# Causal attention in post-layernorm block: the diagonal key tiles of a group are taken between the full ones

## What is computed

```
q = (x @ wq_w.T + wq_b).reshape(b, t, H, HD)      # H = 32, HD = 32
k1, v1 = one key head and one value head
scores = einsum('bqhd,bkd->bhqk', q, k1) / sqrt(HD)
scores = where(causal, scores, -inf)
weights = softmax(scores)
attn = einsum('bhqk,bkd->bqhd', weights, v1).reshape(b, t, H * HD)
x = layernorm(x + attn @ wo_w.T + wo_b)
out = x_sim @ w_sim * (1 / (x_scale * w_scale))   # x and weight scaled to 448 and clipped
x = layernorm(x + out)
```

## Time and profile before

| | us |
|---|---|
| median of 3 runs | 2735.11 |
| lowest, highest | 2733.13, 2735.16 |
| the profiled execution | 2732.4 |
| its span, first to last instruction | 2730.7 |

### The profile page before, as it was taken

One profiled execution on the slowest core, in us unless ns is written; L12 is line 12 of the kernel. 1 busy time (PEld: TensorE's weight loads), 2 busy tenths in 40 slices (PEclk: granted clock), 3 DMA queues, 4 the chain that ended last, 5 costly groups with the idle time before them and its releaser, 6 DMA issues.

```text
span 2730.7 us, 45644 instructions
## 1 busy us (share of the span) xinstructions
PE 2538.9 (93%) x15400; PEld 1587.0 (58%) x15400; DVE 1876.7 (69%) x1432; ACT 1274.1 (47%) x1571; POOL 865.2 (32%) x572
## 2 busy tenths in 40 slices
PE   7999996889999999999888999999999997699998
PEld 5888884545544444444554555444444446588887
DVE  6343335657888889999555778888899993444444
ACT  2222213555566667777335555666677670100000
POOL 2321302424322222122333334222212213466663
PEclk9999997999999999999988999999999998799999
DMA  7343325512111110110333112111101004122221
GB/s 237 118 146 139 115 108 170 137 40 70 39 48 50 47 39 20 31 39 28 86 89 100 51 58 55 44 39 39 39 28 39 29 11 154 49 90 85 92 92 62
DMA packets 78776, 201.47 MB, mean 74 GB/s; under 512 B 8672, under 2 KB 10720, under 8 KB 76512
## 3 DMA queue, kind: packets, MB, share of 16 engines
q1 hardware_dynamic: 51360, 140.01, 17.8%
q10 hardware_dynamic: 27328, 60.30, 5.8%
HBM read 125.83 MB, written 74.45 MB: 73 GB/s over the span
## 4 chain that ended last, share of the span: by engine, by line
PE 77%; issue 7%; DVE 5%; ACT 4%; POOL 3%; DMA 3%; ACTq 1%; SPq 1%; DVEq 0%; POOLq 0%
PE bank L1172 16%; PE bank L1184 15%; PE bank L1083 14%; PE bank L1160 14%; PE bank L1269 13%; ACT prob L703 4%; PE bank L1202 2%; DVE acc L948 2%; DMA q_st<-max_d 2%; PE bank L1194 2%; POOL prob L540 1%; PE bank L1258 1%; DVE acc L945 1%; PE bank L1069 1%; DMA xt_raw<-x_t 1%
## 5 line engine op out<-in xcount | busy, mean ns | idle before, releaser
L703 ACT ACTIVATE prob<-bank 128x1024 f32<-128x1024 f32 (+3 forms) x1280 | 1077.6, 897 | 622.4 <-PE bank L1172 589.7
L948 DVE TENSOR_TENSOR acc<-acc,prob 128x2048 f32<-128x2048 f32 (+3 forms) x512 | 1093.1, 2135 | 130.2 <-POOL prob L540 84.9
L1172 PE MATMUL bank<-q_st,k_st 98*128 98x512 f32 (+3 forms) x2560 | 709.9, 391 | 104.3 <-ACT prob L703 62.5
L1172 PEld LDWEIGHTS bank<-q_st,k_st 98*128 98x128 f32 x2560 | 425.8, 191 | 407.0 <-ACT prob L703 310.0
L1184 PE MATMUL bank<-prob,v_sb 128*32 128x512 f32 (+3 forms) x5120 | 595.9, 547 | 11.0 <-POOL prob L540 10.8
L540 POOL TENSOR_SCALAR_AFFINE_SELECT prob<-prob 128x512 f32<-128x512 f32 x256 | 300.4, 1177 | 882.8 <-ACT prob L703 882.2
L1083 PE MATMUL bank<-xt_hi,w_hi 128*128 128x512 f32 x576 | 228.4, 397 | 16.3 <-DVE xt_lo L790 15.6
L1083 PE MATMUL bank<-xt_hi,w_lo 128*128 128x512 f32 x576 | 227.4, 395 | 0.0
L1083 PE MATMUL bank<-xt_lo,w_hi 128*128 128x512 f32 x576 | 227.3, 395 | 0.0
L1184 PEld LDWEIGHTS bank<-prob,v_sb 128*32 128x32 f32 x5120 | 107.7, 109 | 197.0 <-issue 139.2
L1269 PE MATMUL bank<-wf_hi,xs_hi 128*128 128x512 f32 x512 | 202.5, 396 | 0.0
(11 more groups left out here) (118 smaller groups left out, 2664.9 us busy)
## 6 DMA issues: line engine op xcount, KB each, us to landing
q_st<-q_hi_d SPq DMA_DIRECT2D x128, 256.0 KB
xt_raw<-x_t SPq DMA_DIRECT2D x16, 1024.0 KB, 7.0
q_hi_d<-part_hi ACTq DMA_DIRECT2D x64, 256.0 KB, 2.1
q_lo_d<-part_lo ACTq DMA_DIRECT2D x64, 256.0 KB, 2.3
q_st<-q_lo_d SPq DMA_DIRECT2D x64, 256.0 KB
x<-x_d SPq DMA_DIRECT2D x32, 512.0 KB, 3.2
out<-y ACTq DMA_DIRECT2D x32, 512.0 KB, 2.6
res<-x SPq DMA_DIRECT2D x24, 512.0 KB, 3.4
```

What stands on the lines that cost most here:

```text
L703: nc.scalar.activation(prob[:, t % SLOTS, 2 * p:2 * p + 2, off:NB], bank[:, 2 * p:2 * p + 2, off:NB], ACT.Exp, scale=SCALE).then_inc(p_don ...
L948: nc.vector.tensor_tensor(acc[:, r, :, off:NB], acc[:, r, :, off:NB], new, ALU.add).then_inc(acc_done, 1)
L1172: last = nc.tensor.matmul(bank[:, h, off:NB], k_st[:, t * P:(t + 1) * P], q_st[:, slot, h, off:NB], start=True, stop=True)
```

## The change

`key_order(j)` is a table of the order in which the key tiles of a group are taken. For j = 0 it is as before. For j > 0 the four diagonal tiles get the places 1 + (2i + 1)(n - 2) // 8 of n = 4(j + 1), the full ones fill the rest in their order. A place t now means: scores and weighing read the keys and values of tile `key_order(j)[t]`; the slot, the semaphores and the steps go by the place. `first_query` and the waits for `masked` ask whether the tile at this place is a diagonal one. On POOL the subtraction that gives `att_lo` moves from the head of the pair to behind the second mask of r = 0.

```diff
--- before.py
+++ after.py
@@ -285,9 +285,20 @@
 
             return b * (TT - QT) + (j - 1) * QT + gp
 
+        def key_order(j):
+
+            n = key_tiles(j)
+            places = {1 + (2 * i + 1) * (n - 2) // 8: QT * j + i for i in range(QT)} if j > 0 else {}
+            before = iter(range(n if j == 0 else QT * j))
+            return [places[t] if t in places else next(before) for t in range(n)]
+
+        def diagonal(j, t):
+
+            return key_order(j)[t] - QT * j
+
         def first_query(j, t):
 
-            return P * max(0, t - QT * j)
+            return P * max(0, diagonal(j, t))
 
         def pairs_of_groups(eng, b, body):
 
@@ -527,18 +538,19 @@
                 def body(j, gp, first, last):
                     if j > 0:
                         tile = projected(b, j, gp)
-                        wait_apart(pool, att_hi_cut, tile + 1)
-                        heads = att[:, (j - 1) % 2 * G:(j - 1) % 2 * G + G, bass.ds(gp * P, P)]
-                        nc.gpsimd.tensor_tensor(att_lo[:], heads, att_hi[:].bitcast(F32), ALU.subtract).then_inc(att_cut, 1)
                     for r in range(2):
                         n, s0 = group(b, j, gp, r), step(b, j, gp, r)
                         for i in range(QT):
-                            t = QT * j + i
+                            t = key_order(j).index(QT * j + i)
                             off = first_query(j, t)
                             wait_apart(pool, p_done, s0 * 2 + (2 * t + 4))
                             tri = prob[:, t % SLOTS, :, off:off + P]
                             nc.gpsimd.affine_select(out=tri, in_=tri, compare_op=ALU.is_ge, fill=0.0, base=0,
                                                     pattern=[[0, HG], [1, P]], channel_multiplier=-1).then_inc(masked, 1)
+                            if j > 0 and r == 0 and i == 1:
+                                wait_apart(pool, att_hi_cut, tile + 1)
+                                heads = att[:, (j - 1) % 2 * G:(j - 1) % 2 * G + G, bass.ds(gp * P, P)]
+                                nc.gpsimd.tensor_tensor(att_lo[:], heads, att_hi[:].bitcast(F32), ALU.subtract).then_inc(att_cut, 1)
                         if j > 0 and r == 0:
                             pool.wait_ge(res_in, stored_alone(b, j, gp) * 16 + 16)
                             nc.gpsimd.tensor_tensor(res[:], res[:], bo[:], ALU.add).then_inc(res_ready, 1)
@@ -935,8 +947,8 @@
                             off = first_query(j, t)
                             if t >= 1:
                                 dve.wait_ge(p_done, s0 * 2 + (2 * t + 4))
-                                if t >= QT * j:
-                                    dve.wait_ge(masked, n * QT + (t - QT * j + 1))
+                                if diagonal(j, t) >= 0:
+                                    dve.wait_ge(masked, n * QT + (diagonal(j, t) + 1))
                                 new = prob[:, t % SLOTS, :, off:NB]
                                 if t == 1:
                                     if off > 0:
@@ -1169,7 +1181,7 @@
                     for p in range(2):
                         pe.wait_ge(p_done, s0 * 2 + (2 * t + p + 1))
                         for h in (2 * p, 2 * p + 1):
-                            last = nc.tensor.matmul(bank[:, h, off:NB], k_st[:, t * P:(t + 1) * P], q_st[:, slot, h, off:NB], start=True, stop=True)
+                            last = nc.tensor.matmul(bank[:, h, off:NB], k_st[:, key_order(j)[t] * P:(key_order(j)[t] + 1) * P], q_st[:, slot, h, off:NB], start=True, stop=True)
                         last.then_inc(s_done, 1)
 
                 def weigh_values(n, s0, j, r, t):
@@ -1178,10 +1190,10 @@
                     if t == 0:
                         pe.wait_ge(pv_moved, n + 1)
                     pe.wait_ge(p_done, s0 * 2 + (2 * t + 4))
-                    if t >= QT * j:
-                        pe.wait_ge(masked, n * QT + (t - QT * j + 1))
+                    if diagonal(j, t) >= 0:
+                        pe.wait_ge(masked, n * QT + (diagonal(j, t) + 1))
                     for h in range(HG):
-                        last = nc.tensor.matmul(bank[h * HD:(h + 1) * HD, 4 + r, off:NB], v_sb[:, t], prob[:, t % SLOTS, h, off:NB],
+                        last = nc.tensor.matmul(bank[h * HD:(h + 1) * HD, 4 + r, off:NB], v_sb[:, key_order(j)[t]], prob[:, t % SLOTS, h, off:NB],
                                                 start=(t == 0), stop=(t == key_tiles(j) - 1), skip_group_check=True)
                     last.then_inc(pv_done, 1)
 
```

## The result

The median after is 2769.61 us (four runs, 2765.29 to 2770.87), the median before 2734.40 (four runs, 2733.13 to 2735.16; three of them are those of the table ahead of the prediction): a ratio of 1.0126, 95% interval 1.0109 to 1.0144. The change makes the kernel 1.3% slower. The profiled execution of after took 2768.89 us, 36.5 more than that of before.

A forecast was written before the change was run, and what follows sets the result against it. PE bounds the kernel, with about 4 us of waiting per pair that an order can change. j = 3 +6.0, j = 2 +16.8, j = 1 +5.4, together +28: 2760.6 us profiled, median 2763, range 2734 to 2785.

The forecast's parts named there:

- (1): Start of each group: the wait from second scores to first weighing is a chain of 3.42 us; no change.
- (2): j = 2 and 3, r = 1: the 128-column diagonal tile weighed in a step without projection; +0.7 us a pair.
- (3): r = 0, 384-column diagonal tile beside ACT's copy of att_hi: +0.5 us a pair in j = 3, +0.2 in j = 2.
- (4): Start of r = 0, j = 2: DVE's reciprocal late for PE's spreading, +1.2 us a pair; no wait in j = 3.
- (5): j = 1: mask wait of 1.0 us goes, reciprocal late; net +0.1 in r = 0, +0.8 in r = 1.
- (6): Ends of the two batches: DVE's last sum and maximum end sooner, -0.7 us each.
- (7): att_lo moved behind two masks, outside j = 1: it waits for the same copy as before; 0.
- The first pairs of j = 1: First pair of each batch: long waits perhaps hidden or lengthened; taken as 0, bounds -5 to +5 us for both.
- the ring of D3: Next scores wait for both exponentials; the 128-column tile's short weighing between makes PE wait 0.80 us without projection.
- Faster: Rival, chance 0.13: last mask leaves the group's end, DVE's work is spread, reciprocals come before PE asks; 2723 us.
- No change: Rival, chance 0.10: PE's work is the same and ring waits only move; within 5 us, 2735 us.
- Much slower: Rival, chance 0.17: masks and sums exclude each other so often that DVE sets the pace; 2780 us.

## Why the prediction was right, and where its terms were off

The forecast was 2763 with a range of 2734 to 2785; 2769.61 lies in it, 6.6 us above the forecast, on the slower side as forecast. The profiled execution took 36.5 us more where my terms make 28. The mechanism is the right one in the main; where single terms were wrong and their sum still came near, I call it luck. Point by point:

**(1) Group starts.** As a chain, right. From the second scores of a group to its first weighing 3.43 us pass after and 3.42 before.

**(2) D3 in a bare step, +0.7.** Right in mechanism and size for j = 3: one moved tile brought 0.7 (81.11 to 81.82) and the distance 2.76 stands in the trace. In the changed kernel, counted on PE as above, r = 1 is longer than before by 0.8 in j = 3 and by 0.97 in j = 2. But "none where three or more projection matmuls stand there too" doesn't quite hold. This line of after is such a place, with three matmuls between D3's weighing and the scores:

```profile
1221.75 0.30 PEld L1184 LDWEIGHTS bank<-q_st,k_st 98*128 98x128 f32 x2 [0.29 <-ACT prob L715]
```

The four scores matmuls it belongs to take 1.22 us there, where the earlier trace rows have 1.09: 0.1, a small cost.

**(3) D1 at the copy, +0.2 and +0.5.** Right: 0.2 and 0.4.

**(4) The late reciprocal, +1.2 in j = 2.** Present, and too large: 0.7. The chain was the right one, but its parts weigh otherwise. I put the cause mainly at the full tile behind the statistics, VectorE's backlog. Taking 1.05 us out of that backlog made PE's wait 0.25 shorter and won nothing in all, since PE then waits for the mask of D2; moving the mask of D0 from between the two sums made the step 0.58 shorter and won 0.47. In j = 3 "no wait" held for steady pairs (3.17 us in the step of the spreading, 3.29 before), but not for the first pair of a stage, which takes 3.89 there.

**(5) j = 1, +0.1 in r = 0 and +0.8 in r = 1.** The sum was near (+0.9 forecast, +1.05 to 1.2 measured), its halves were not: +0.5 to 0.6 in either. The mask wait of 1.04 went and the reciprocal's wait came, 1.01 in r = 0 as forecast, 0.62 in r = 1. Missing in r = 0 was the mask of D2 behind att_lo: "done some 2 us before its weighing" was wrong, PE waits 0.35 for it in this pair (621.60), and less in the next ones. att_lo runs beside sums and is longer than I took it for in this pair (3.91 us at 617.04, 2.37 in the next one). That the reciprocal's wait is what costs in j = 1 is read from the trace: no run takes it away there.

**(6) Batch ends, -0.7 each.** The sign was wrong. At the end of the first batch, after:

```profile
1349.64 1.27 PE L1206 MATMUL bank<-acc,head_col 128*32 128x128 f32 x32 [2.59 <-DVE acc L960]
```

PE's wait there did fall by 0.7, from 3.29 to 2.59, but the line itself comes 45.21 us after the first exponential of the last r = 1, against 44.53 before: +0.7, not -0.7. VectorE ends that chain, and its sums behind the statistics are these, after:

```profile
1341.72 0.68 DVE L934 TENSOR_TENSOR res<-bank,res 128x512 f32<-128x512 f32 x1
...
1344.17 5.35 DVE L960 TENSOR_TENSOR acc<-acc,prob 128x512 f32<-128x512 f32 x3
```

and before:

```profile
1326.28 0.68 DVE L922 TENSOR_TENSOR res<-bank,res 128x512 f32<-128x512 f32 x1
...
1328.72 3.75 DVE L948 TENSOR_TENSOR acc<-acc,prob 128x1536 f32<-128x1536 f32 x3
```

The statistics start 0.9 sooner, counted from the same exponential (37.29 against 38.21), but D3 and two full tiles follow them instead of D1, D2 and D3: 5.35 against 3.75, 1.6 more. I had counted the tiles that came earlier and not the full ones that took their place at the end. To the first exponential of what follows it is +1.4 (110.56 to 111.99). The other 0.7 can't be laid at the order's door: the kernel with D0 early in j = 1, whose j = 3 is that of before, takes 111.2 over the same stretch, while the 44.53 and 45.21 repeat to some 0.03 in it and in both batches.

**(7) att_lo later.** 0 for att_lo itself, but the masks now behind it are late, see (5).

**The first pairs of j = 1**, taken as 0 with bounds of 5, moved by +0.6 and +0.2. The first of them lasts 59.6 to 62.1 us in the runs that keep masks and the order of after in j = 1, so this says little.

**Where the missing 8 us are.** All in j = 3 (in the rest +1.7, -0.4 and -1.4 nearly cancel). In the first batch my terms make 3.0 us, and 7.5 were measured. The first three pairs and r = 0 of the last took +2.0, +1.6, +1.6 and +0.9, 6.1 together where I had 3.7 (three times 1.1, and 0.4); the rest took +1.4 where I had -0.7. So 2.4 are the steps inside the pairs, set too small (0.4 of it the reciprocal of the first pair), and 2.1 the end, of which 1.4 are term (6) with its sign turned and 0.7 may be chance. Inside a pair of j = 3, r = 1 took +0.8 where I had 0.7, and r = 0 took +0.8 where I had 0.4: the mask of D2 behind att_lo, which (7) put at nothing, is 0.24 of that. In j = 2 the forecast of 2.1 met the measured 2.2 partly by luck: the reciprocal is 0.7 instead of 1.2, the copy 0.2, the mask of D2 0.1, and what is left, 1.2, is more than the 0.7 that the ring of D3 explains. I take the rest, 0.5 in j = 2 and some 0.3 in j = 3, for the ring at further steps, but no run measured it: its cause stays open.

**The rivals.** *Faster* decided on the reciprocal ending before PE asks. It doesn't: the waits view gives, for PE's matmuls at the spreading, first after, then before,

```profile
PE bank L1214 <- DVE r_den L921: 21.2, 27, 1.6
```

```profile
PE bank L1202 <- DVE r_den L909: 2.9, 2, 1.8
```

in total us, times and longest. *No change* falls with the interval. *Much slower* falls with the pair of kernels without masks. Its premise is right all the same: masks and att_lo last far longer beside sums here (2.69 and 4.52 us, last view of the first section). The Trainium skill ("SBUF — State Buffer", Who interferes with whom) says that a VectorE instruction with two SBUF inputs contends with a GpSimd instruction that reads SBUF; the trace agrees. But these long instructions are mostly not what PE waits for.

## What to carry to other kernels

When a small work item moves out of a tail, look at what its neighbours leave on the other engine: in a two-stage ring a short item behind a long one costs the difference (0.7 us here), while a tail that shrinks on both engines at once cost almost nothing. Before moving anything, follow what must be ready at the start of the next round, for a tail of short items may also be what lets the slower engine catch up: the two runs that moved D3 alone both made PE wait longer for the reciprocal (1.17 and 1.40 us in j = 2). And at an end count what takes the place of the moved item, not only the item; the gain that was to be had (some 8 of 10 us) lay in one tile of one stage whose wait the trace named.

## What was not expected of the hardware

- A mask or an att_lo that starts while a VectorE sum runs behaves here as if it waited for the sum's end and then took about its usual time. Of the masks of after that start inside one sum, those of 1.00, 1.78 and 2.69 us all end 0.50 us behind it; one in the open takes 0.64. att_lo takes 2.33 in the open, 2.52 where the sum ends 0.28 behind its start, and 4.50 where it ends 2.27 behind it. A VectorE sum behind a mask shows 0.62 idle each time.
- A PE wait can be paid twice. In the kernel with all diagonal tiles under the projection, after the wait of 1.96 us, the granted clock fell; over its windows of pairs in j = 2 and 3 it is 0.95 to 0.98, not 1.00:

```profile
1227.00:1232.00 5.00, 4.74 (x24) 2.58 (x24) 4.61 (x3) 1.42 (x2) 5.00 (x4) 0.66 0.00 0
```

  0.66 is a mean between the full level (2.4 GHz) and the lower one (1.2 GHz); in the windows of pairs shown here it is 1.00, but for the two of 69 us (0.95), where PE also waited long at the cut (2.71 us in the first of them).
- The turn of a loop costs an engine time that its neighbour in the queue can hide: about 0.8 us of branch and register instructions on VectorE, seen only when the instruction ahead of them shrank from 1.22 to 0.17 us, which is why that won 0.24. A short instruction alone doesn't do it: at 820.83 of the same trace one of 0.21 us (L781) is followed at once by a sum.
